# Decoder of two layers: the last norm taken row by row in the second cross-attention's loop, its power on GpSimd

## The reference, cut to what matters

```python
x = x + _L1_xattn_ref(_layernorm(x), ctx_1024, ctx_1024, Wq, Wk, Wv, mask)   # one head, masked softmax over 361
x = x + _L1_ffn_ref(_layernorm(x), w_gate, w_up, w_down)

def _layernorm(x, axis=-1, eps=1e-05):
    m = jnp.mean(x, axis=axis, keepdims=True); v = jnp.var(x, axis=axis, keepdims=True)
    return (x - m) / jnp.sqrt(v + eps)

def _L1_ffn_ref(x, ...):
    x = act_qdq(x)          # scale = max|x| over the WHOLE tensor / 32767, then round
    ...
def act_qdq(x):
    scale = jnp.maximum(jnp.max(jnp.abs(x)) / qmax, 1e-12)
    return jnp.clip(jnp.round(x / scale), -qmax - 1.0, qmax) * scale
```

## Time and profile before

| | us |
|---|---|
| median of 3 runs (1441.37 to 1446.31) | 1442.63 |
| the profiled execution's own time | 1443.37 |
| its span | 1441.2 |
| TensorE busy | 1271.4 (88%) |
| VectorE busy | 1044.2 (72%) |
| ScalarE busy | 740.2 (51%) |
| GpSimd busy | 249.8 (17%) |

### The profile page before, as it was taken

The page is one execution under the profiler, slowest core; times in us unless marked ns, Lnnn a source line. Parts: engine busy times, 40 slices in busy tenths (PEclk is TensorE's granted clock), DMA queues, the critical chain, the costliest instruction groups (busy, mean ns, idle before and its releaser), DMA issues.

```text
span 1441.2 us, 27742 instructions
## 1 busy us (share of the span) xinstructions
PE 1271.4 (88%) x9826; PEld 1080.2 (75%) x9826; DVE 1044.2 (72%) x2596; ACT 740.2 (51%) x1811; POOL 249.8 (17%) x306
## 2 busy tenths in 40 slices
PE   5999899978999999999999999999799978969319
PEld 5889888867787877878787787877577756759218
DVE  5975767555667777777777777777589867885974
ACT  5542424244655565555556555555356643436472
POOL 2343444435000000000000000000054430000100
PEclk9999999989999999999999999999799989989759
DMA  9100101041000000000000000000100022300001
GB/s 283 58 1 7 38 1 44 1 160 36 1 11 12 11 12 10 10 1 10 11 10 11 10 10 1 10 1 2 48 12 2 2 67 75 97 0 1 0 0 46
DMA packets 34547, 40.66 MB, mean 28 GB/s; under 512 B 4889, under 2 KB 29066, under 8 KB 34442
## 3 DMA queue, kind: packets, MB, share of 16 engines
q1 hardware_dynamic: 33614, 39.24, 9.0%
q10 hardware_dynamic: 828, 0.14, 0.1%
HBM read 35.36 MB, written 4.01 MB: 27 GB/s over the span
## 4 chain that ended last, share of the span: by engine, by line
PE 51%; DVE 17%; issue 5%; ACT 4%; POOL 1%; DVEq 0%; ACTq 0%; POOLq 0%
PE bank L759 8%; PE bank L761 7%; PE bank L760 7%; PE bank L976 4%; PE bank L960 4%; PE bank L968 3%; PE bank L936 3%; ACT prob L1636 2%; DVE amax L2462 2%; DVE nmx L2278 2%; PE bank L1209 1%; PE bank L1227 1%; DVE kTl L2050 1%; PE bank L997 1%; PE bank L1241 1%
## 5 line engine op out<-in xcount | busy, mean ns | idle before, releaser
L1636 ACT ACTIVATE prob<-bank,nmx 100x361 f32<-100x361 f32 x256 | 142.6, 560 | 156.8 <-DVE nmx L2278 155.9
L2278 DVE TENSOR_REDUCE nmx<-bank 100x1 f32<-100x361 f32 x256 | 124.2, 526 | 22.6 <-PE bank L960 15.7
L688 POOL TENSOR_TENSOR frstd<-fmoments,eps 100x1 f32<-100x1 f32 x32 | 6.2, 192 | 648.9 <-DVE fmoments L2221 648.8
L759 PE MATMUL bank<-cxTh,wxkh 128*128 128x362 f32 x256 | 100.0, 391 | 2.8 <-DVE kTl L2050 2.8
L976 PEld LDWEIGHTS bank<-pT,vv 128*64 128x64 f32 (+1 forms) x1536 | 71.2, 139 | 37.5 <-issue 28.2
L976 PE MATMUL bank<-pT,vv 128*64 128x100 f32 (+1 forms) x1536 | 96.6, 261 | 1.9 <-DVE oTl L2049 1.8
L2295 DVE TENSOR_SCALAR prob<-prob,rsum 100x361 f32<-100x361 f32 x256 | 92.9, 405 | 4.5
L968 PE MATMUL bank<-ident,prob 100*128 100x100 f32 (+1 forms) x768 | 90.7, 254 | 1.6 <-DVE prob L2295 1.6
L2049 DVE TENSOR_TENSOR oTl<-bank,oTh 128x100 fp32r<-128x100 f32 x128 | 32.9, 257 | 81.4 <-ACT oTh L1622 78.1
L968 PEld LDWEIGHTS bank<-ident,prob 100*128 100x128 f32 (+1 forms) x768 | 85.5, 153 | 7.1 <-DVE prob L2295 2.6
L1622 ACT CAST oTh<-bank 128x100 fp32r<-128x100 f32 x128 | 31.8, 249 | 112.6 <-PE bank L976 112.4
(11 more groups left out here) (395 smaller groups left out, 3778.5 us busy)
## 6 DMA issues: line engine op xcount, KB each, us to landing
cx<-in_ctx_dram SPq DMA_DIRECT2D x32, 128.0 KB, 2.0
xc<-in_ctx_dram SPq DMA_DIRECT2D x32, 128.0 KB
parked_weights<-parking SPq DMA_DIRECT2D x9, 256.0 KB, 5.5
mask_i<-in_mask_BxS_ik_dram SPq DMA_DIRECT2D x16, 141.0 KB
w<-in_L_attn_W_dram SPq DMA_DIRECT2D x2, 1024.0 KB, 13.8
cx<-in_ctx_dram SPq DMA_DIRECT2D x16, 105.0 KB, 2.0
xc<-in_ctx_dram SPq DMA_DIRECT2D x16, 105.0 KB
x<-in_x_dram SPq DMA_DIRECT2D x4, 400.0 KB
```

What stands on the lines that cost most here:

```text
L759: pe.matmul(o, wh, mh, start=start, stop=False)
L1636: nc.scalar.activation(prob[:, h % 4, :], bank[S_BANKS[e]][0:T, 0:S], ACT.Exp, bias=nmx[:, h:h + 1], accum_out=psum_[:, h:h + 1]).then_inc ...
L2278: nc.vector.tensor_reduce(nmx[:, h:h + 1], bank[S_BANKS[e]][0:T, 0:S], AX_X, ALU.max, negate=True).then_inc(xa_max, 1)
```

## The change

Each row is normalised in the loop, one slot after its update, instead of all rows behind it. In `dve_slot`, the statistics of the updated row go to the small tiles `stats` and `moments` (one place for each r), and the aggregate follows at once and raises `ff_v`. GpSimd, behind its weight splits, adds eps and takes the power -0.5 for each row in turn and raises `ff_r`. At the head of VectorE's next slot (`step(4)`) the new `row_widest` waits for that, writes the normalised row to `zq`, and reads its largest absolute value from it. Row 15 has its `row_widest` behind the loop. The reductions of the raw row, the sixteen aggregates, ScalarE's square root, the small operations on the sixteen maxima and `rows_normalized` go. A round has 5 links a slot instead of 3.

```diff
--- before.py
+++ after.py
@@ -722,6 +722,13 @@
                 nc.gpsimd.tensor_copy(high[:], w[:]).then_inc(f1_w, 1)
                 pool.wait_ge(f1_w, 2 * n + 1)
                 nc.gpsimd.tensor_tensor(low[:], w[:], high[:].bitcast(F32), ALU.subtract).then_inc(f1_w, 1)
+            for c in range(B):
+                links += 1
+                r = c % G
+                pool.wait_ge(ff_v, 2 * B + c + 1)
+                nc.gpsimd.tensor_tensor(rstd[:, r:r + 1], moments[:, r, 1:2], eps[0:T, :], ALU.add).then_inc(pool_link, 1)
+                pool.wait_ge(pool_link, links)
+                nc.gpsimd.tensor_tensor(rstd[:, r:r + 1], rstd[:, r:r + 1], minus_half[0:T, :], ALU.pow).then_inc(ff_r, 1)
             pool.wait_ge(f1_ca, 2 * TILES)
             nc.gpsimd.tensor_copy(dnh[:], wdown[:]).then_inc(f1_w, 1)
             pool.wait_ge(f1_w, 5)
@@ -1786,7 +1793,6 @@
             in_slots(act, act_slot)
 
 
-            all_deviations(TURN[3])
             def rows_high(g):
                 for k in range(KD):
                     act.wait_ge(ln_t, 2 * KD * NG + KD * g + k + 1)
@@ -2416,9 +2422,20 @@
             norm(2)
 
 
+            def row_widest(c, o):
+
+                dve.wait_ge(ff_r, 2 * B + c + 1)
+                row = zq[:, ds(c, 1), :].rearrange("p a d -> p (a d)")
+                link(nc.vector.tensor_scalar(row, x[:, ds(c, 1), :].rearrange("p a d -> p (a d)"), moments[:, o, 0:1],
+                                             rstd[:, o:o + 1], ALU.subtract, ALU.mult))
+                return nc.vector.tensor_reduce(widest_row[:, ds(c, 1)], row, AX_X, ALU.max, apply_absolute_value=True)
+
             def dve_slot(g, r):
 
                 step = steps(g, r)
+                there, c, o = step(4)
+                if there:
+                    row_widest(c, o)
                 there, c, o = step(1)
                 if there:
                     dve.wait_ge(x1_mask, c + 1)
@@ -2440,9 +2457,10 @@
                     nc.vector.scalar_tensor_tensor(row, bank[7][0:T, 0:D], rsum2[:, o:o + 1], row, ALU.mult,
                                                    ALU.add).then_inc(x1_x, 1)
                     dve.wait_ge(x1_x, c + 1)
-                    row_stats(c)
-                    nc.vector.tensor_reduce(widest_row[:, ds(c, 1)], row, AX_X, ALU.max)
-                    nc.vector.tensor_reduce(lowest_row[:, ds(c, 1)], row, AX_X, ALU.min)
+                    nc.vector.memset(pause[:, 2:3], 0.0)
+                    link(nc.vector.bn_stats(stats[:, o, :], row))
+                    nc.vector.memset(pause[:, 3:4], 0.0)
+                    nc.vector.bn_aggr(moments[:, o, :], stats[:, o, :]).then_inc(ff_v, 1)
                 there, c, o = step(0)
                 if there:
                     dve.wait_ge(xc_in[r], 16 * (NS + 1) * g + 16 * (NS + 1))
@@ -2450,7 +2468,7 @@
                     nc.vector.tensor_scalar(mask_n[:, o], mask_f[:, o], 1.0, -MASK_FILL, ALU.subtract,
                                             ALU.mult).then_inc(x1_mask, 1)
 
-            in_slots(dve, dve_slot, lambda g: chain.rounds(g, NG - 1, 3 * G, 1))
+            in_slots(dve, dve_slot, lambda g: chain.rounds(g, NG - 1, 5 * G, 1))
             dve.wait_ge(x1_x, B)
 
 
@@ -2492,29 +2510,12 @@
                 link(nc.vector.tensor_scalar(unit_e12, unit, 1e12, None, ALU.mult))
                 return unit, unit_e12
 
-            link(nc.vector.memset(pause[:, 3:4], 0.0))
-            for b in range(B):
-                ins = nc.vector.bn_aggr(moments_all[:, b, :], stats_all[:, b, :])
-            ins.then_inc(var_ready, 1)
-            dve.wait_ge(var_ready, TURN[3])
-            mean = moments_all[:, :, 0]
             nc.vector.memset(ones_all[:], 1.0)
             nc.vector.memset(sc[:, 40:41], ROUND)
-            link(nc.vector.memset(sc[:, 41:42], -ROUND))
-            nc.vector.tensor_tensor(widest_row[:], widest_row[:], mean, ALU.subtract)
-            link(nc.vector.tensor_tensor(lowest_row[:], mean, lowest_row[:], ALU.subtract))
-            link(nc.vector.tensor_tensor(widest_row[:], widest_row[:], lowest_row[:], ALU.max))
-            dve.wait_ge(std_ready, TURN[3])
-            link(nc.vector.reciprocal(rstd_all[:], std_all[:]))
-            link(nc.vector.tensor_tensor(widest_row[:], widest_row[:], rstd_all[:], ALU.mult))
+            nc.vector.memset(sc[:, 41:42], -ROUND)
+            link(row_widest(B - 1, G - 1))
             link(nc.vector.tensor_reduce(amax[0:T, 56:57], widest_row[:], AX_X, ALU.max))
             to_diagonal(0, T)
-            def rows_normalized(g):
-                for b in range(G * g, G * g + G):
-                    ins = nc.vector.tensor_scalar(zq[:, b, :], x[:, b, :], moments_all[:, b, 0:1], rstd_all[:, b:b + 1],
-                                                  ALU.subtract, ALU.mult)
-                return ins
-
             def rows_quantized(g):
                 part = zq[:, G * g:G * g + G, :]
                 link(nc.vector.tensor_scalar(part, part, sc[0:T, 16:17], ROUND, ALU.mult, ALU.add))
@@ -2526,12 +2527,9 @@
                     cols = slice(N * g, N * (g + 1))
                     rest(zTl[:, k, cols], bank[Z_BANKS[g] + k][:, 0:N], zTh[:, k, cols]).then_inc(ln_done, 1)
 
-            link(rows_normalized(0))
             scales(0, T, 1.0, 1e12)
             rows_quantized(0)
             for g in range(NG):
-                if g + 1 < NG:
-                    link(rows_normalized(g + 1))
                 rows_low(g)
                 if g + 1 < NG:
                     rows_quantized(g + 1)
```

## The result

The changed kernel takes 1451.73 us (median of 10 runs, 1449.79 to 1456.56), the kernel before 1442.81 us on the same chip (10 runs, 1441.21 to 1446.31). The ratio is 1.0062, with an interval of 1.0048 to 1.0075: slower by 8.9 us. The forecast was 1450.4 us, in a range of 1446 to 1455.5.

The account below looks back on a forecast made before the run. VectorE was taken to bound three of every four loop slots, TensorE the other. The profiled 1443.37 us plus 7.0 for ten slots at 0.70 and 0 for drain and tail gave 1450.4, range 1446 to 1455.5.

Parts of the forecast that it names:

- Who leads: Second cross-attention's loop: TensorE leads 6.97 us of each group of four slots, VectorE the other 13.42; period 20.39 us.
- The first rival: TensorE bounds the loop after all, VectorE's 2.8 us a group fit into its 2.9: 1443.4 us, not slower; 8%.
- The chain to the normalisation: From row update through aggregate, GpSimd's addition and power to row_widest: start at 2.28 us, after a wait of 0.36.
- The rest of the slot: From row_widest's normalisation (0.44 us) through its reduction (0.33) to the next mask multiply at 3.05, plus 0.04 for registers.
- a slot's price: Extra time of a slot that VectorE leads: 0.70 us, with bounds of 0.30 and 1.11, or 1.15 with registers.
- How many pay: Of 15 slots with row_widest, 10 pay in full, 7.0 us; those in slot 0 fit into TensorE's lead.
- Drain and tail: Stretch behind the loop: diagonal 0.6 us later, 0.4 less behind it; sum +0.2, taken as 0, 1 us either side.
- Each for the other's whole instruction: Rival: in the slots GpSimd and VectorE stop for each other's whole instructions, 1.15 us a slot, 1454.9 us; 17%.
- one sign of being wrong: The prediction is wrong if the granted clock falls below 1.00 between 1200 and 1270.
- The rival: The granted clock falls in the loop as TensorE idles 0.70 us more a slot: up to 1471 us; 4%.

Follow-up runs that it names:

- the one with the power in the loop: Kernel before, with each row's aggregate and GpSimd's power made in the loop, raw-row reductions kept and no row normalised there: 1444.45 us, ratio 1.0009.

## Why the prediction was right

It was right in the sign, in the mechanism and nearly in the size: 1450.4 against 1451.73. Some of that closeness is luck. The difference was forecast at 7.0 us and measured at 8.9, and the base of the sum, the profiled execution, lies 0.6 above the median of the kernel before. Inside the traced stretch two errors partly cancel: the slots cost 0.8 us more than forecast, drain and tail 0.35 less. Step by step:

- **Who leads.** Shown by the experiments with less and with more on VectorE: less shortens the loop (no normalisation, 4.61 us a slot; the copy moved, 4.29), more lengthens it (4.91, 5.53, 6.15). The first rival, TensorE with 2.9 us to spare beside it, fell. VectorE was busy 17.10 of 20 us and full in three slots of four.
- **The chain to the normalisation.** Forecast 0.36 us of wait, found 0.53. The statistics started at 0.53 behind the update instead of 0.65, so the aggregate was at 0.99 instead of 1.11 and VectorE reached its wait earlier, which lengthens the wait and costs nothing. Aggregate to normalisation was 1.32 us instead of the 1.17 of the earlier trace rows: addition 0.26 later as there, power 0.28 behind it (0.34 there) but 0.66 long (0.54), and the normalisation 0.12 us behind its end (0.03 there). The two errors cancel to 0.03: normalisation at 2.31, forecast 2.28.
- **The rest of the slot.** From normalisation to reduction 0.55 us, where I had 0.44 and 0.04 for the registers; in the tail, without registers, it is 0.45 (1279.29 to 1279.74 of the variant with row_widest last). The loop addresses its row through a register and the tail doesn't; 0.10 us is probably the price of that, though no run took it alone. From reduction to multiply 0.34, forecast 0.33. The mis-sized term of the sum is this one: a slot's price was 0.81, not 0.70.
- **How many pay.** Ten, as counted; the two behind slot 0 of groups 2 and 3 came for nothing, with 0.19 us of room left in the wait before the copy. Row 1 to row 13 is 7.80 us longer; forecast 7.0.
- **Drain and tail.** Forecast 9.86 us from row 13's update to the diagonal and, less 0.42, counted as 0 in sum; found 9.35 (9.28 before) and -0.42 behind it, so -0.35 in sum. Row 13 to 15 took 6.15, not 6.50.
- **Each for the other's whole instruction.** The Trainium skill, "SBUF — State Buffer", section on the ports that VectorE and GpSimd share, would have the later of the two block fully until the other's instruction is done. Beside GpSimd's small operations the mask operations took 0.32 and 0.35 us, no longer than before the change (0.34, 0.35), and the power 0.66 instead of 0.55: a hold-up of 0.11 us, not of an instruction, and the price of 1.15 us fell. How long the power takes goes with how much of the mask operation is left when it starts: 0.26 us in the changed kernel, 0.12 in the one with the power in the loop, where it took 0.55. That would fit a wait for VectorE's end that hides behind the power's own start. But in the latter kernel the addition, begun 0.04 us earlier, ran beside the second mask operation for 0.15 us with neither longer, which a full block would not allow as it stands:

```profile
1260.78 0.19 POOL L729 TENSOR_TENSOR rstd_all<-moments,eps 100x1 f32<-100x1 f32 x1
1260.82 0.35 DVE L2461 TENSOR_SCALAR mask_n<-mask_f 100x361 f32<-100x361 f32 x1
1261.05 0.55 POOL L732 TENSOR_TENSOR rstd_all<-rstd_all,minus_half 100x1 f32<-100x1 f32 x1
```

For the long operation of the earlier trace rows the rule holds; for the short ones these traces neither follow it in full nor show no hold-up, and which part of an instruction holds the other stays open.
- **The clock.** By its letter one sign of being wrong came true: in 1200 to 1220 the granted clock was 0.94. That is the end of a dip around the second score product (0.50 during it, from 1197.38, after 4.04 us idle; 1.00 again from 1204), ahead of row 0's update and of all that the change touches; the kernel before has it too, a little earlier (0.57 in 1194 to 1198). From 1204 to 1280 it was 1.00. The rival needed only one more power.

**What stays open.** The medians lie 8.9 us apart (8.7 the second time), the traced stretch explains 7.0 to 7.45. The interval of the ratio, 6.9 to 10.8 us, holds that, so 1.2 to 1.9 us are unexplained, if they are there. The kernels of this study reached the first mask multiply between 1185.8 and 1195.02 us, the changed kernel at 1195.02 and, profiled again, at 1194.82, later than all others. A shift that comes with the program as a whole, ahead of the changed part, is therefore possible. Two things speak against it. The kernel with two powers, longer than the changed one by a GpSimd instruction for each row, had its first score product at 1186.93, where the kernel before had it at 1186.97 (the changed kernel 1191.28 and 1190.49). And two executions of one and the same kernel, the one before with the copy moved, had it at 1188.62 and 1184.26, 4.4 us apart. Single profiled executions can't settle it.

## What to carry to other kernels

An engine that is 85% busy can be full: look for an idle time between its rows before counting room on it, and price a slot by the distance between two like instructions. Before a wait on a short chain over another engine is put at the head of a slot, place it where other work of one's own already stands between: moving row_widest behind the mask operations took all of the 7 us back. And when an engine leads, look at what it does that an idler one could do: one copy given to ScalarE was worth 0.4 to 0.5%, more than anything the norm's rearrangement could bring. But look where such a gain arises before calling it the loop's: in the two traces 1.9 us of it lie in loop and drain, and 3.9 to 4.5 in the first slots, where the copy no longer stood behind an operation that GpSimd held up.

## What the runs showed of the hardware

- The small power of GpSimd (100x1) took 0.55 us with VectorE still, 0.66 beside VectorE's mask operations, in the changed kernel and in the one with two powers; I had expected either no effect or a whole instruction's. It took 0.55 where only 0.12 us of the mask operation were left when it started.
- One long operation beside another can hold a whole pipeline's start: 3.47 us of one mask operation became 4.75 us of TensorE idling in front of its second score product, since an unrelated copy was queued behind it.
- Idle time in TensorE can have a second price. In the changed kernel the granted clock stayed 1.00 from 1204 to 1280; with two powers, and waits of up to 1.79 us before the score product, it was 0.92 in 1222 to 1242 and a score product took 2.72 us instead of 1.45. But the same wait did not always bring it: with two powers, 1.65 us of waiting stood before a score product of 2.42 us (at 1221.47) and before one of 1.43 (at 1246.20). So it is in the tail. The maximum's product took 0.72 us at a granted clock of 0.50 after 4.91 us idle. After 3.81 us idle it took 0.44 us at 1.00 with row_widest last (first fence), and 0.72 us at 0.50 with the copy on ScalarE as well (second). How long TensorE sat idle just before does not decide it alone:

```profile
1280.81 0.44 PE L1350 MATMUL bank<-diagonal,ones_all 100*128 100x100 f32 x2 [3.81 <-DVE diagonal L2485]
```

```profile
1269.82 0.72 PE L1350 MATMUL bank<-diagonal,ones_all 100*128 100x100 f32 x2 [3.81 <-DVE diagonal L2483]
```
